# Two-layer graph attention on one core: VectorE takes a step's maximum ahead of the weighing, and the product follows eight steps behind the scores

## What is computed

```python
def _gat_layer(x, W, adj):
    proj = x @ W
    Wh, Ws = jnp.split(proj, 2, axis=-1)
    scores = Wh @ Ws.T
    a = jax.nn.softmax(scores, axis=-1) * adj
    out = a @ Wh
    out = out + x
    return jax.nn.leaky_relu(out, 0.01)
x0 = x
for l in range(2):
    x = _gat_layer(x, W_stack[l], adj)
return layernorm(x0 + x)
```

## Time and profile before

| | us |
|---|---|
| median of 3 runs | 1690.79 (1690.45 to 1693.78) |
| the profiled execution | 1689.17 |
| its span, first to last instruction | 1687.3 |
| PE busy | 1594.6 (95%) |
| PE weight loads busy | 1324.0 (78%) |
| DVE busy | 1231.2 (73%) |
| ACT busy | 676.5 (40%) |
| POOL busy | 916.3 (54%) |

### The profile page before, as it was taken

One profiled execution on the slowest core, in us unless ns is written; L12 is line 12 of the kernel. 1 busy time (PEld: TensorE's weight loads), 2 busy tenths in 40 slices (PEclk: granted clock), 3 DMA queues, 4 the chain that ended last, 5 costly groups with the idle time before them and its releaser, 6 DMA issues.

```text
span 1687.3 us, 23469 instructions
## 1 busy us (share of the span) xinstructions
PE 1594.6 (95%) x8104; PEld 1324.0 (78%) x8104; DVE 1231.2 (73%) x1558; ACT 676.5 (40%) x1175; POOL 916.3 (54%) x935
## 2 busy tenths in 40 slices
PE   7889999999999999999688999999999999999996
PEld 6778888888788888888577888888888888878785
DVE  4667777767777777777535788778878887788785
ACT  4244444444444444444323443444343444443442
POOL 2355555555555555555353555555555655555565
PEclk9999999999999999999889999999999999999999
DMA  5357767787678777777713677777777777767774
GB/s 181 85 144 184 196 184 183 184 206 184 183 181 198 184 184 186 190 190 208 215 55 91 175 186 191 197 187 190 189 196 202 188 193 196 191 180 187 194 204 130
DMA packets 167750, 302.59 MB, mean 179 GB/s; under 512 B 39760, under 2 KB 68432, under 8 KB 167504
## 3 DMA queue, kind: packets, MB, share of 16 engines
q1 hardware_dynamic: 106192, 133.28, 32.4%
q0 software_dynamic: 36864, 134.23, 27.9%
q10 hardware_dynamic: 24576, 33.59, 8.3%
HBM read 157.29 MB, written 9.44 MB: 99 GB/s over the span
## 4 chain that ended last, share of the span: by engine, by line
PE 58%; DVE 20%; POOL 7%; ACTq 6%; ACT 5%; issue 3%; DMA 1%; SPq 0%; POOLq 0%
PE banks L410 19%; PE banks L309 10%; PE banks L311 9%; PE banks L310 9%; PE banks L412 9%; DVE neg_max L601 7%; DVE ring L629 6%; POOL a_lo L727 6%; ACTq L215 6%; DVE ring L634 4%; ACT a_hi L522 3%; ACT ring L503 1%; DVE weight L620 1%; DVE wh L565 1%; DVE x_t L565 1%
## 5 line engine op out<-in xcount | busy, mean ns | idle before, releaser
L727 POOL TENSOR_TENSOR a_lo<-turned,a_hi 128x512 fp32r<-128x512 f32 x512 | 716.9, 1416 | 687.4 <-ACT a_hi L522 687.1
L410 PE MATMUL banks<-wh,a_hi 128*128 128x512 f32 x2048 | 754.8, 407 | 56.0 <-POOL a_lo L727 49.4
L503 ACT ACTIVATE ring<-banks,neg_max 128x1024 f32<-128x1024 f32 x256 | 286.0, 1117 | 798.4 <-DVE neg_max L601 798.4
L412 PE MATMUL banks<-wh,a_lo 128*128 128x256 f32 x2048 | 578.4, 282 | 0.0
L410 PEld LDWEIGHTS banks<-wh,a_hi 128*128 128x128 f32 x2048 | 388.7, 190 | 189.8 <-POOL a_lo L727 85.8
L601 DVE TENSOR_REDUCE neg_max<-banks 128x1 f32<-128x1024 f32 x256 | 311.0, 1215 | 270.0 <-PE banks L311 270.0
L309 PE MATMUL banks<-x_t,q_t 128*128 128x512 f32 x1024 | 406.1, 397 | 5.6 <-DVE x_t L565 4.0
L311 PE MATMUL banks<-x_t,q_t 128*128 128x512 f32 x1024 | 402.5, 393 | 0.0
L310 PE MATMUL banks<-x_t,q_t 128*128 128x512 f32 x1024 | 401.4, 392 | 0.0
L412 PEld LDWEIGHTS banks<-wh,a_lo 128*128 128x128 f32 x2048 | 390.9, 191 | 6.1
L629 DVE SCALAR_TENSOR_TENSOR ring<-ring,weight,load 128x1024 f32<-128x1024 f32 x256 | 372.3, 1454 | 4.9 <-DMA load<-adj 2.4
(11 more groups left out here) (66 smaller groups left out, 743.1 us busy)
## 6 DMA issues: line engine op xcount, KB each, us to landing
load<-adj POOLq DMA_DIRECT2D x256, 512.0 KB, 5.0
turned<-ring SPq DMA_DIRECT2D x1536, 64.0 KB, 4.0
turned<-ring ACTq DMA_DIRECT2D x512, 64.0 KB, 4.1
ring<-x SPq DMA_DIRECT2D x8, 512.0 KB, 4.9
rows<-x SPq DMA_DIRECT2D x32, 128.0 KB, 4.1
x_scratch<-rows SPq DMA_DIRECT2D x32, 128.0 KB, 4.0
ring<-x_scratch SPq DMA_DIRECT2D x8, 512.0 KB, 4.9
rows<-x_scratch SPq DMA_DIRECT2D x32, 128.0 KB, 4.3
```

What stands on the lines that cost most here:

```text
L410: nc.tensor.matmul(psum[:, bank, :], a_hi[:, s, b], wh[:, k].rearrange("p a d -> p (a d)"), start=start, stop=stop, skip_group_check=True)
L412: last = nc.tensor.matmul(psum[:, bank, 0:D], a_lo[:, s, b], wh[:, k, 0], start=False, stop=stop, skip_group_check=True)
L503: nc.scalar.activation(ring[:, i % RING, :].rearrange("p (b e) -> p b e", b=2), psum[:, 2 * (i % 2):2 * (i % 2) + 2, :], ACT.Exp, bias=neg ...
L727: nc.gpsimd.tensor_tensor(a_lo[:, j % 2].rearrange("p b (r j) -> p b r j", r=QUADS), as_f32(turned[:, unit % 2, :, b:b + SUB, :]).rearrang ...
```

## The change

The weighing and turning of chunk s-4 go behind the maximum of chunk s in DVE's step, and so do the x splits; normalising, finishing and statistics of rows go ahead of it. ACT's two moves of a chunk go from the end of a step to the next one, behind its splits. POOL's inversion goes ahead of its load. The product lags eight steps, and the layers are one step further apart.

```diff
@@ -36,9 +36,9 @@
     PAIRS = TILES // 2
     WPAIRS = TILES // 2
     LAG_WEIGH = 4
-    LAG_PRODUCT = 7
+    LAG_PRODUCT = 8
     LAG_ROWS = 13
-    OFFSET = CHUNKS + 4
+    OFFSET = CHUNKS + 5
     LAG_LAST_ROWS = CPT + LAG_PRODUCT
     STEPS = OFFSET + CHUNKS + LAG_LAST_ROWS + 3
     LATE_GROUP = OFFSET + 3
@@ -544,6 +544,9 @@
                 if k is not None:
                     split_a(2 * k)
                     split_a(2 * k + 1)
+                m = chunk_at(step - LAG_WEIGH - 1)
+                if m is not None:
+                    move_blocks(m)
                 for side in sides_before(step):
                     split_side(side)
                 if step == LATE_GROUP:
@@ -553,9 +556,6 @@
                 i = chunk_at(step)
                 if i is not None:
                     exponentials(i)
-                m = chunk_at(step - LAG_WEIGH)
-                if m is not None:
-                    move_blocks(m)
                 for side in sides_after(step):
                     split_side(side)
 
@@ -685,12 +685,12 @@
                 late = step == LATE_GROUP
                 if ready is not None:
                     row_weights(ready)
-                if late:
+                if whole is not None:
+                    normalise_rows(whole)
+                if done is not None:
                     finish_rows(done)
-                i = chunk_at(step - LAG_WEIGH)
-                if i is not None:
-                    weigh(i)
-                    turn_blocks(i)
+                if of_stats is not None:
+                    row_stats(of_stats)
                 for side in sides_after(step - 1):
                     if comes_later(side):
                         split_side(side)
@@ -698,20 +698,18 @@
                     split_side(side)
                 if late:
                     split_x(2 * GROUPS - 1)
-                for g in x_groups_at(step):
-                    split_x(g)
                 i = chunk_at(step)
                 if i is not None:
                     chunk_max(i)
+                i = chunk_at(step - LAG_WEIGH)
+                if i is not None:
+                    weigh(i)
+                    turn_blocks(i)
+                for g in x_groups_at(step):
+                    split_x(g)
                 for side in sides_after(step):
                     if not comes_later(side):
                         split_side(side)
-                if whole is not None:
-                    normalise_rows(whole)
-                if done is not None and not late:
-                    finish_rows(done)
-                if of_stats is not None:
-                    row_stats(of_stats)
 
         @block.gpsimd
         def _(pool):
@@ -763,14 +761,14 @@
                 if k is not None:
                     split_a(2 * k)
                     split_a(2 * k + 1)
-                m = chunk_at(step - LAG_WEIGH)
-                if m is not None and m + 2 < LAYERS * CHUNKS:
-
-                    pool.wait_ge(a_done, m + 1)
-                    load_adj(nc.gpsimd, m + 2)
                 whole = normalise_at.get(step)
                 if whole is not None:
                     invert_std(whole)
+                m = chunk_at(step - LAG_WEIGH)
+                if m is not None and m + 2 < LAYERS * CHUNKS:
+
+                    pool.wait_ge(a_done, m + 1)
+                    load_adj(nc.gpsimd, m + 2)
 
 
 # ---- launch: one core; inputs and output as the reference has them ----
```

More of the change, by code:

```diff
@@ L765, in _ @@
                     split_a(2 * k + 1)
+                whole = normalise_at.get(step)
+                if whole is not None:
+                    invert_std(whole)
                 m = chunk_at(step - LAG_WEIGH)
@@ L770, in _ @@
                     load_adj(nc.gpsimd, m + 2)
-                whole = normalise_at.get(step)
-                if whole is not None:
-                    invert_std(whole)
 def kernel(x, adj, L0_gnn_W_stack):
```

## The result

The changed kernel takes **1809.32 us**, the median of 4 runs (1805.81 to 1818.22), beside 1692.28 for the kernel before on the same chip: a ratio of 1.0696, with a 95% interval of 1.065 to 1.0743. That is slower, by 117 us where the prediction had 53, and 7 us beyond the upper end of its range.

What follows compares the result with a forecast made beforehand. TensorE was taken to nearly set the pace, at 12.00 us a pair; with the change the ring would add 52 us and the rest net +1: +53 on 1689.2 is 1742, by the median 1744 us, range 1650 to 1802.

Steps and rivals of the forecast that it cites:

- the ring: Six chunk slots: exponentials wait until moves of six chunks before have landed; the new bound, +52 us, chance 0.61.
- Pair >= 4.68 + X: Two steps last at least 4.68 us, from even exponentials to SyncE's first move, plus X.
- X: Time from an even chunk's first move issue to its last landing, taken as 7.6 us, ends 6.8 and 8.2.
- The floor of 11.53: Time in us of a pair of steps without waits, worked out from single steps of the kernel before.
- 12.44 against 12.00: Forecast against present us per pair of steps: 4.84 + 7.6 = 12.44, +0.44 over 118 pairs, +52 us.
- The price put on the load's place: An adjacency load issued among an even chunk's moves, not beside the first, costs them 0.7 to 0.9 us.
- this holds one maximum of four back by about 1.1 us: Layer 2: inversion behind splits and normalising ahead of the maximum delay it; 0 taken, up to 16 us.
- Row sums: On VectorE, these, q's low half and row weights ahead of the maximum fill idle time; 0 taken.
- Net +1, ends -5 and +8: Us for fill, drain, the stretch between the layers and the end after the last scores, together.
- row stores and loads: In SyncE's queue they stand between even and odd moves, where it now waits for lo_done; 0 taken.
- the 94% foretold in both: Sign of being right: TensorE's busy share falls to some 94% in the steady stretches, from 98%.
- Rival C: Weighing gets between the two a_lo, load goes beside the first move: 12.72 us a pair, +85, 1777; chance 0.14.

Runs made afterwards that it cites:

- e10: The changed kernel with seven ring slots, VectorE's row operations last, x loads between the layers and adjacency loads one step earlier and later respectively: 1650.81 us, 0.9761.
- e3: The changed kernel with normalising, finishing and statistics of rows put back behind the weighing, at the end of VectorE's step: 1723.25 us, 1.0181.
- e9: e3 with each adjacency load one step later in GpSimd's program, directly behind an a_lo pair: 1736.86 us, 1.0256.
- e4: The changed kernel with GpSimd's inversion put ahead of its a_lo pair: 1726.47 us, 1.0193.
- e6: The changed kernel with SyncE's loads of x groups 10 to 14 between the layers issued one step earlier: 1794.00 us, 1.0609.
- e1: The kernel before with VectorE's new order alone and the inversion ahead of the load, product lag still seven: 2096.21 us, 1.2395.

## Why the prediction was right and wrong

**Right: the ring as the mechanism in layer 1. The direction was luck in the main:** the ring brought some 5 of the 117 us, and the rest came from places where the prediction had put 0 or little. "Pair >= 4.68 + X" held: 4.72 to the first move, even exponentials 12.15 apart, the landing 0.1 us or so ahead of the exponentials six chunks on. The floor of 11.53 was reached by e10. For the tile's change: the weighing is 1316 ns on the mean from 1454, the wait for the factor 10.4 us from 48.4.

**A size off: X and what the ring costs.** X was taken as 7.6 and is 7.28 on the mean, 7.44 by the median, over layer 1's window; by the mean, 4.84 + 7.28 is 12.12, and the pair is 12.20. I set 12.44 against 12.00, +26 us a layer. Measured in layer 1: 585.40 - 574.17 = +11 in the 96 steady steps, and 8 of it given back at the layer's ends, in its first 24 chunks, where the prediction had no gain. Layer 2 without the loop (e3) is +1 on the whole. So the ring's term was 52 and came to about 5 net. In layer 1 the exponentials did wait for moves in nearly every pair (57 times), so the term that was mis-sized is X, which went from 5.1 to 8.4 us there by where the load fell, and the gain at the start. The price put on the load's place, 0.7 to 0.9 us more behind the first move than beside it, was refuted by e9; in the chunks whose load came behind the sixth issue X was 2.4 less.

**Failed: "this holds one maximum of four back by about 1.1 us ... 0 taken, up to 0.5 us in each of 32 tiles, 16 us".** The inversion behind the splits and the normalising ahead of the maximum cost 77 us in layer 2 (74 by e4). I counted the inversion's 0.57 us and one delay, with the ring as its cover, and never followed the order of waits around: normalise waits for the inversion, the inversion for the a_lo pair, the pair for the load, and the load for the weighing, which is now behind the normalising. That is a cycle through two queues, and it sets a pace of its own (26.9 us a tile) once it is longer than four steps of the ring (24.4 at 12.2 a pair). The cover is then gone, for ScalarE waits for the maximum, not for the ring.

**Failed: "Row sums ... come ahead of the maximum: VectorE is idle 150 of 574 us ... at that place; 0".** They are not idle time filled: the load, which now waits for the weighing, put a_lo right behind every weighing, and so beside the small operations, whose mean went from 164 to 1173 ns (L613) and from 446 to 2030 (L658). e3, which moves all but the row weights back, has 294 and 449. What they cost apart from the loop no run shows.

**Failed: "Net +1, ends -5 and +8" for fill, drain and middle, with "on SyncE, row stores and loads ... 0".** The middle is +26.6 and the tail +8.8. I looked at the row transfers in SyncE's queue and not at the x loads, which stand there too and have TensorE, ScalarE and the moves behind them. e6 shows 20 of the 27. The tail was not tried by a run.

**By its own signs:** TensorE's share went to 97% in layer 1 and 89% in layer 2, for the 94% foretold in both; exponentials waiting for moves came mostly in layer 1; product matmuls waiting over 80 us for a_lo (137.3), but largely through layer 2's loop. The one sign that named layer 2's loop, maxima late behind L670, wasn't on my list.

## What to carry to other kernels

When a wait, or a step that is waited for, moves ahead in one queue, follow it around until it comes back: a cycle through two or three queues has a pace of its own, which no single duration shows, and it is compared with the loop that bounds the kernel now. An operation that costs nothing where it stands behind the critical one of its engine may cost several times its duration ahead of it. Move with a reordered step only what needs to move: here the rows' work ahead of the maximum and the a_lo pair behind the load's wait cost time, and with them put right, the x loads earlier and one more buffer, the kernel with the maximum ahead of the weighing was 2.4% faster than the kernel before. That the maximum's place is what earned it was not shown.

## What the runs showed of the hardware that wasn't expected

**A small operation can wait out two of GpSimd's.** From the timeline of after, VectorE's row and then GpSimd's:

```profile
1219.68 2.25 DVE L613 TENSOR_TENSOR scaled_sum<-factor,chunk_sum 128x4 f32<-128x4 f32 x1
```

```profile
1219.40 2.51 POOL L725 TENSOR_TENSOR a_lo<-turned,a_hi 128x512 fp32r<-128x512 f32 x2
```

An operation on 128x4 elements, 164 ns long in the kernel before, started 0.28 us into an a_lo pair and ended 0.02 after it, not after the first of the two. Of the 32 that were held in after, 31 ended behind the second a_lo; in e10 the 34 that came during a first a_lo all ended behind that one. L658 in the chain above waited out a pair too (2.53 us for 446 ns). At a tile's change before, the weighing also got in between the earlier trace rows. The Trainium skill (SBUF, State Buffer, section on who interferes with whom) has the lock held by an instruction to its end, and then the other engine would get its turn between the two; the trace agrees in e10 and before, and in after it doesn't. What decides it is open. Where the operation starts bears on it: over all fourteen traces, the 151 of this line that waited for the second a_lo all started 0.28 to 0.37 us into the first; of the 82 that ended behind the first, 23 started there too and 59 elsewhere. Rival C rested on that turn between the two, so a rule taken from one row was less safe than it looked.

**A load's place among small moves goes with how long they take.** Six moves of 64 KB, issued over 3.1 us with one load of 512 KB near them, landed 5.1 us after the first issue when the load was issued behind the sixth, 7.4 with it 1.3 to 2.5 us behind the first, 8.6 with it 2.5 to 3.0 behind (medians of after), and 5.8 with it up to 1.0 us ahead (e1). These are the loads' places as they fell in two traces; no run moved the load alone to the cheap ones, so that it is the cause was not tried.
